# Edge passes of a graph kernel: three eight-slot loop bodies and one four-slot body with their own buffers, in place of one eight-slot body

## The chip, the cores and the metric

One Trainium2 chip, one of its cores. The metric is device time in microseconds (us) of one execution; lower is better. Time before: 10095.14 us, the median of 3 runs (10087.63 to 10098.26).

## What is computed

Four graph layers run one after the other on 3125 nodes of width 128 and 103125 directed edges (`src`, `dst`, sorted by `dst`), in fp32. All need, for each node, a weighted sum over the rows of the nodes that point at it:

```python
# layer 0: relation-aware attention; keys get the embedding of the edge's type (64 types)
# layer 1: three rounds of GAT convolution, 8 heads of 16
e = leaky_relu(e_src[src] + e_dst[dst], 0.2)
w = exp(e - segment_max(e, dst)[dst])
out = segment_sum(h[src] * (w / segment_sum(w, dst)[dst]), dst) + b
# layer 2: attention whose scores take features of the edge (64 attributes, a distance)
# layer 3: a sum of neighbours, scaled by 1/sqrt(degree) on both sides
```

Ahead of each layer stands a normalisation, behind it a residual sum.

## The kernel before

The nodes are sorted by degree and cut into NB = 25 blocks of 128, one node per partition. The edges of a block stand in *slots*: slot s of partition p is the s-th incoming edge of node p. A block has as many slots as its busiest node has edges, rounded up to 8. The chunk of work is SLOTS = 8 slots, that is 8 x 128 edges, in two halves of HALF = 4. Chunk boundaries by block stand in `bounds` (made at lines 499 to 526), at least 2 chunks per block and 3 in the last. The index lists are in DRAM: `el_idx`, `el_msk`, `el_typ`, one entry per chunk (written at lines 884 to 997).

`edge_pass` (from line 1542) is called six times: pass 0 (layer 0), passes 1 to 3 (the convolutions), pass 4 (layer 2) and pass 5 (layer 3). A pass reads a table of node rows in DRAM and writes the next table. Each engine runs a loop of its own over blocks and chunks, tied to the others by semaphores:

- **SP** (SyncE) loads the indices of a half, line 1582, `idx` h, when the gathers of the chunk before have landed; in pass 0 also the types (1587), in pass 4 `first` (1591) and the mask (1595).
- **POOL** (GpSimd) waits for the indices (1554) and for the half's landing buffer to be free (1556), then issues 4 indirect gathers (1558), each one row per partition; in pass 4 one gather of features per chunk (1565). Behind the gathers of block b it issues the scatter of block b-1's new rows (1444).
- **ACT** (ScalarE) copies the landed half into `work` (1384, 1391, 1402), which needs `work_free`, frees the landing buffer, and does the exponential (1285). In its chunk loop `step` (1671) the order is: one-hot of the types of chunk j+1 (`act_onehot`, 1368 and 1374, pass 0 only), exponential of chunk j, copy of chunk j+1. In passes 1 and 2 it also turns a tile of edge features per block (804 to 840), inside the first step of the next block.
- **PE** (TensorE) in pass 0 makes the keys of a half in `make_k` (1728): four matmuls of one-hot and type embeddings (1738) and one that adds the gathered keys (1743); it does so one chunk ahead of VectorE. At a block's end it does the projections (1071, 1074).
- **DVE** (VectorE) does the scores (1299, 1303 in passes 0 and 4; 1324, 1326 in 1 to 3), the running maximum (1273), the shift (1275), the weighing (1289) and the sum over slots (1294), after which the chunk's result is in slot 8 of `work`. At a block's end follow normalisation, projection and the new table rows (1151 to 1260).

There is one set of landing buffers (`land0`, `land1`, `land2`, two halves each), of `idx` (two halves), `first`, `msk` and `feat`. So the gathers of a half of chunk j+1 wait until ACT (or, in pass 5, DVE at 1358) has taken the same half of chunk j.

ACT's chunk step before:

```python
def step(j):
    if types: act_onehot(act)
    act_weights(act)
    act_copy(act, j + 1, landed)
```

## Time and profile before

| What | Value |
|---|---|
| median of the runs | 10095.14 us |
| the profiled execution | span 10072.8 us |
| POOL busy | 5899.5 us (59%) |
| DVE busy | 4386.1 us (44%) |
| PE, ACT busy | 1840.1 us (18%), 1435.6 us (14%) |
| granted TensorE clock | 1.00 throughout |
| DMA | 560.52 MB, mean 56 GB/s |
| first gather of passes 0 to 5 at | 920.5, 2572.4, 4049.4, 5507.1, 7015.9, 8706.1 us |
| last instruction | 10067.8 us |
| gathers, line 1558 | 5568, which is 6 passes x 116 chunks x 8 |

The span is one profiled execution from the first to the last instruction; the runs are timed on their own and their median is 22 us above it. Busy time counts instructions on an engine, not the waits between them, so no share here is a bound by itself; the passes are 91% of the span.

### The profile page before, as it was taken

How to read it: one execution, taken by the hardware profiler on the slowest of the kernel's cores; microseconds unless marked ns; L12 is line 12 of the kernel's file. 1: busy time of each engine (PE TensorE's matmuls, PEld its weight loads, DVE VectorE, ACT ScalarE, POOL GpSimd, SP SyncE). 2: the span in 40 equal slices, each digit the busy share in tenths (PEclk: the TensorE clock that was granted, in tenths of full speed). 3: DMA queues.
4: the chain of work that ended last, by engine and by line, in shares of the span. 5: the costliest groups of instructions: out<-in, count | busy, mean ns of one | idle time of the engine just before them, and what ended most of it. 6: DMA issues, size and time to landing. Idle time of an engine off the chain costs nothing. (4 is left out here: it accounts for less than half of the span.)

```text
span 10072.8 us, 74038 instructions
## 1 busy us (share of the span) xinstructions
PE 1840.1 (18%) x8000; PEld 1190.9 (12%) x8001; DVE 4386.1 (44%) x9101; ACT 1435.6 (14%) x3285; POOL 5899.5 (59%) x5959
## 2 busy tenths in 40 slices
PE   4334666666111111011111000000000000000000
PEld 4232333333000111000011000000000000000000
DVE  9314555555444444344444444444344444322222
ACT  0210222222111111111111111111111111000000
POOL 0113656555566666666666666665666665566666
DMA  0232434434333323323323322222312222222222
GB/s 17 38 48 52 99 96 99 97 93 97 51 58 57 57 57 61 53 57 58 57 60 57 48 47 48 49 47 41 43 43 43 42 46 40 39 47 46 48 45 44
DMA packets 612542, 560.52 MB, mean 56 GB/s; under 512 B 465184, under 2 KB 477759, under 8 KB 612390
## 3 DMA queue, kind: packets, MB, share of 16 engines
q0 software_dynamic: 205232, 477.48, 25.1%
q1 hardware_dynamic: 372836, 42.79, 3.2%
q10 hardware_dynamic: 34449, 40.02, 1.4%
q14 instruction: 21, 0.16, 0.0%
q8 instruction: 4, 0.07, 0.0%
HBM read 535.16 MB, written 24.61 MB: 56 GB/s over the span
## 5 line engine op out<-in xcount | busy, mean ns | idle before, releaser
L1558 POOL DMA_INDIRECT land<-table,idx x5568 | 5535.7, 994 | 3181.0 <-issue 1681.7
L1294 DVE TENSOR_REDUCE work<-prod 128x136 f32<-128x1224 f32 x464 | 1089.6, 2348 | 67.8 <-DVE prod L1289 0.2
L1071 PE MATMUL bank<-ident,hid 128*128 128x128 f32 x175 | 78.1, 446 | 4874.0 <-issue 2764.6
L1289 DVE TENSOR_TENSOR prod<-work,wt 128x1224 f32<-128x1224 f32 x464 | 665.5, 1434 | 639.5 <-DVEq L1279 410.6
L1391 ACT ACTIVATE work<-land 128x576 f32<-128x576 f32 x696 | 475.1, 683 | 2311.7 <-DMA land<-table,idx 2029.9
L1358 DVE TENSOR_REDUCE land<-land 128x128 f32<-128x640 f32 x232 | 285.7, 1231 | 1018.9 <-DMA land<-table,idx 830.9
L1324 DVE TENSOR_TENSOR sc<-work,own 128x64 f32<-128x64 f32 x348 | 81.2, 233 | 1327.2 <-issue 550.3
L1071 PEld LDWEIGHTS bank<-ident,hid 128*128 128x128 f32 x175 | 31.8, 182 | 5032.1 <-issue 5032.1
L1738 PE MATMUL bank<-rel,onehot 64*128 64x128 f32 x1856 | 511.7, 452 | 358.6 <-PEq L1736 278.0
L1738 PEld LDWEIGHTS bank<-rel,onehot 64*128 64x128 f32 x1856 | 449.9, 324 | 655.4 <-issue 655.4
L1743 PE MATMUL bank<-land,ident 128*128 128x512 f32 x464 | 481.0, 1140 | 108.3 <-DMA land<-table,idx 103.6
L1284 ACT ACTIVATE sc<-top 128x8 f32<-128x8 f32 x580 | 120.9, 208 | 2435.0 <-ACTq L1283 1651.9
L1299 DVE TENSOR_TENSOR kk<-work,own 128x512 f32<-128x512 f32 x232 | 160.8, 693 | 542.9 <-DVEq L1334 271.7
L1303 DVE TENSOR_REDUCE sc<-kk 128x32 f32<-128x512 f32 x464 | 318.3, 686 | 42.4 <-DVE kk L1299 0.8
L1299 DVE TENSOR_TENSOR kk<-bank,own 128x512 f32<-128x512 f32 x232 | 160.5, 692 | 379.2 <-DVEq L1314 194.5
L1444 POOL DMA_INDIRECT table<-stage,stage_i x150 | 149.2, 994 | 272.5 <-POOLq L1443 235.9
L1402 ACT ACTIVATE work<-land 128x512 f32<-128x512 f32 x232 | 145.5, 627 | 697.8 <-DMA land<-table,idx 647.8
L1384 ACT ACTIVATE work<-land 128x544 f32<-128x544 f32 x232 | 149.7, 655 | 591.7 <-DMA land<-table,idx 366.4
L363 POOL DMA_INDIRECT info_d<-inf,rank_i x25 | 24.2, 970 | 347.4 <-POOLq L361 340.1
L820 PE MATMUL bank<-b_ft,ones 1*125 1x176 f32 x150 | 69.4, 563 | 816.7 <-PEq L818 668.2
L870 POOL DMA_INDIRECT rec<-rec_id,at_i x25 | 23.7, 949 | 309.9 <-POOLq L869 309.9
L1273 DVE TENSOR_REDUCE top<-sc 128x8 f32<-128x72 f32 x580 | 162.3, 280 | 32.9
(285 smaller groups left out, 3855.0 us busy)
## 6 DMA issues: line engine op xcount, KB each, us to landing
land<-table,idx POOLq DMA_INDIRECT x5568
typ<-el_typ SPq DMA_DIRECT2D x232, 128.0 KB
attr<-in_edge_attr ACTq DMA_DIRECT2D x75, 343.8 KB
idx<-el_idx SPq DMA_DIRECT2D x1392, 2.0 KB
rec_ft<-fts ACTq DMA_DIRECT2D x75, 85.9 KB
near<-dist_t ACTq DMA_DIRECT2D x75, 62.5 KB
table<-stage,stage_i POOLq DMA_INDIRECT x150
first<-el_idx SPq DMA_DIRECT2D x116, 1.0 KB
```

Of the source, the lines that this page charges most:

```text
L1273: dve.tensor_reduce(top[:], sc[:].rearrange("p s h -> p h s"), AX.X, ALU.max).then_inc(ch.semaphore, ch.one())
L1289: dve.tensor_tensor(prod[:].rearrange("p s (h v) -> p s h v", h=HEADS), work[:, :, 0:HV].rearrange("p s (h v) -> p s h v", h=HEADS), wt[:] ...
L1294: dve.tensor_reduce(work[:, SLOTS, 0:HV], prod[:].rearrange("p s c -> p c s"), AX.X, ALU.add).then_inc(ch.semaphore, ch.one())
L1299: dve.tensor_tensor(kk[h][:], keys, slots(queries, HALF), ALU.mult).then_inc(ch.semaphore, ch.one())
L1303: dve.tensor_reduce(sc[:, h * HALF:(h + 1) * HALF, :], kk[h][:].rearrange("p s (h d) -> p s h d", h=HEADS), AX.X, ALU.add).then_inc(ch.sem ...
L1358: dve.tensor_reduce(land2[1 - h][:, HALF, :], land2[h][:].rearrange("p s c -> p c s"), AX.X, ALU.add).then_inc(ch.semaphore, ch.one())
L1384: act.activation(work[:, h * HALF:(h + 1) * HALF, 0:HV], land0[h][:, :, D:W0], ACT.Copy).then_inc(s(f"rows_free{h}"), 1)
L1391: act.activation(work[:, h * HALF:(h + 1) * HALF, :], land1[h][:], ACT.Copy).then_inc(s("act_chain"), 1)
L1444: pool.indirect_dma_start(target, bass.IndirectOffsetOnAxis(ap=stage_i[0:rows].bitcast(U32), axis=0), stage[0:rows], None).then_inc(s("tab ...
L1558: pool.indirect_dma_start(rows[h][:, k, :], None, source, bass.IndirectOffsetOnAxis(ap=idx[h][:, k:k + 1].bitcast(U32), axis=0)).then_inc( ...
L1738: last = pe.matmul(ps_rel[h][:, k * D:(k + 1) * D], onehot[mine, :, k], rel[mine], start=k == 0, stop=False, skip_group_check=True)
L1743: pe.matmul(ps_rel[h][:].rearrange("p (s d) -> p s d", d=D), ident[:], rows[h][:, :, 0:D], start=False, stop=True, skip_group_check=True). ...
```

## The change

The passes are walked with four loop bodies instead of one. Each has its own `idx`, `first`, `msk`, `feat` and landing buffers and its own semaphores:

- bodies a, b and c take 8 slots, body d takes 4 (the second half's place in `work`, `sc` and `prod`, so its DVE and ACT instructions cover 4 slots plus the running one);
- a block's slots are rounded up to 4, at least 28. With q = slots/4 - 7, the pair a, b runs (q>>2)+1 times, c ((q>>1)&1)+1 times, d (q&1)+1 times. Every block therefore takes a, b, c, d, and some repeat c, d or the pair. The counts are made on the device once (`quads`, `turns_at`) and read from SBUF by each engine at every block.
- ACT's order per body is one-hot, copy, exponential, with nothing for the body after it; the feature work of passes 1 and 2, and `act_after` in pass 3, stand behind the last body of a block. PE makes the keys of a block inside that block and no longer ahead; its feature work stands ahead of the block's projection.
- SP reloads `idx` of a body when ACT (DVE in pass 5) tells that it has seen the gathers landed, where it used to wait for the landing itself; PE too is told by ACT (`keys_in`).
- Pass 5 reduces each half into `part` and adds it to `acc`, where it used to take the running sum as a fifth slot.
- Setup gets some twelve small DVE instructions and four matmuls more, and one instruction more per run of 64 slots.

```diff
+        BODIES = {"a": (0, 1), "b": (0, 1), "c": (0, 1), "d": (1,)}
+        PLACES = [(x, q) for x, qs in BODIES.items() for q in qs]
+        idx = {(x, q): sb(f"idx_{x}{q}", [P, HALF], I32) for x, q in PLACES}
...
+        land = {(x, q): sb(f"land_{x}{q}", [P, HALF * W0]) for x, q in PLACES}
...
+        def turns_of(engine, b):
+
+            q = engine.value_load(quads[0:1, bass.ds(b, 1)], min_val=FEWEST, max_val=2 * JMAX) - FEWEST
+            return ((q >> LOOP_SHIFT) + 1, ((q >> (LOOP_SHIFT - 1)) & 1) + 1) + (((q & 1) + 1,) if TAIL_HALF else ())
+
+        def walk(engine, b, body):
+
+            loops = zip([("a", "b"), ("c",), ("d",)], turns_of(engine, b))
+            for bodies, turns in loops:
+                with engine.Fori(0, turns):
+                    for x in bodies:
+                        body(x)
+
+        def walk_numbered(engine, b, body):
+
+            at = [engine.value_load(turns_at[0:1, n, bass.ds(b, 1)], min_val=0, max_val=JMAX) for n in range(3 if TAIL_HALF else 2)]
...
+        def act_landed(act, x, h, t):
+
+            act.wait_ge(landed(x, h), t * (16 * HALF) + 16 * HALF)
+            act.sem_inc(s(f"idx_free_{x}{h}"), 1)
...
+        def act_copy_l0(act, x, t):
+            for h in BODIES[x]:
+                act_landed(act, x, h, t)
+                act.sem_inc(s(f"keys_in_{x}{h}"), 1)
             act.wait_ge(s("work_free"), 1)
             act.sem_inc(s("work_free"), -1)
...
+                    with sp.Fori(0, NB) as b:
+                        j0 = sp.value_load(bounds[0:1, bass.ds(b, 1)], min_val=0, max_val=JMAX - 2 * RC)
+                        t = turns_of(sp, b)
+                        with sp.Fori(0, t[0]) as i:
+                            loads("a", j0 + i * 2)
+                            loads("b", j0 + i * 2 + 1)
+                        with sp.Fori(0, t[1]) as i:
+                            loads("c", j0 + t[0] * 2 + i)
+                        if TAIL_HALF:
+                            with sp.Fori(0, t[2]) as i:
+                                loads("d", j0 + t[0] * 2 + t[1], i)
...
-                        def step(j):
+                        def body(x, t):
                             if types:
-                                act_onehot(act)
-                            act_weights(act)
-                            act_copy(act, j + 1, landed)
...
+                                act_onehot(act, x)
+                            act_copy(act, x, t)
+                            act_weights(act, x)
+
+                        def block_end(b, more):
+
+                            if makes_features:
+                                act_copy_turned(act, 0)
+                                if more:
+                                    act_attr_load(act, 0, makes_features + b + 1)
+                                act_store_features(act, 0, makes_features + b)
+                            if act_after:
+                                act_after(act)
...
+                        with act.Fori(0, NB - 1) as b:
+                            walk_numbered(act, b, body)
+                            block_end(b, True)
...
+                        with pe.Fori(0, NB) as b:
                             if types:
+                                walk(pe, b, make_k)
                                 pe_project(pe, wo0[:], D)
+                            if makes_features:
+                                pe_turn_edges(pe, 0)
+                                pe_features(pe, 0)
+                            pe_after(pe)
```

## Rows read from the trace of the kernel before

**Rows 1.** The page's costliest groups: line engine op, tensors, count | busy us, mean ns | idle before

```profile
L1558 POOL DMA_INDIRECT land<-table,idx x5568 | 5535.7, 994 | 3181.0 <-issue 1681.7
```

**Rows 2.** The waits of POOL, one row per pass, passes 0 to 5: total us, times, longest

```profile
POOL land L1558 <- POOLq L1556: 376.5, 91, 7.1
...
POOL land L1558 <- POOLq L1556: 202.4, 38, 10.3
...
POOL land L1558 <- POOLq L1556: 173.4, 40, 9.1
...
POOL land L1558 <- POOLq L1556: 247.8, 32, 11.0
...
POOL land L1558 <- POOLq L1556: 256.9, 65, 12.7
...
POOL land L1558 <- POOLq L1556: 119.0, 29, 7.1
```

**Rows 3.** The tile sh in pass 0: duration min/median/max ns, first and last start

```profile
L1275 DVE TENSOR_TENSOR sh<-sc,top x116: 232/232/234, 936.8 to 2549.8; 128x72 f32<-128x72 f32 x116
```

**Rows 4.** Timeline of pass 0, one body: start us, us, engine line op, count [idle before]

```profile
1352.53 2.20 PE L1738 MATMUL bank<-rel,onehot 64*128 64x128 f32 x8 [3.47 <-PEq L1736]
...
1357.33 2.20 PE L1738 MATMUL bank<-rel,onehot 64*128 64x128 f32 x8 [0.60 <-PEq L1736]
...
1358.92 0.71 ACT L1368 ACTIVATE typ_d<-typ,neg_p 128x512 f32<-128x512 f32 x1
...
1359.47 2.07 PE L1743 MATMUL bank<-land,ident 128*128 128x512 f32 x2
1359.89 0.63 ACT L1374 ACTIVATE onehot<-typ_d 128x512 f32<-128x512 f32 x1 [0.27 <-ACTq L1373]
...
1362.47 0.69 DVE L1299 TENSOR_TENSOR kk<-bank,own 128x512 f32<-128x512 f32 x1 [0.18 <-DVEq L1314]
...
1364.34 0.23 DVE L1275 TENSOR_TENSOR sh<-sc,top 128x72 f32<-128x72 f32 x1
...
1364.87 0.25 ACT L1285 ACTIVATE wt<-sh 128x72 f32<-128x72 f32 x1
```

**Rows 5.** Timeline of pass 1, end of a block and start of the next

```profile
3990.47 0.25 ACT L1285 ACTIVATE wt<-sh 128x72 f32<-128x72 f32 x1
...
4001.51 0.32 ACT L837 ACTIVATE fts<-bank 125x176 f32<-125x176 f32 x1 [0.55 <-issue]
4002.10 0.31 ACTq L840 DMA_DIRECT2D rec_ft<-fts  x1
...
4008.43 0.25 ACT L1285 ACTIVATE wt<-sh 128x72 f32<-128x72 f32 x1
...
4013.53 0.23 DVE L1324 TENSOR_TENSOR sc<-work,own 128x64 f32<-128x64 f32 x1 [0.66 <-DVEq L1323]
...
4014.36 0.23 DVE L1275 TENSOR_TENSOR sh<-sc,top 128x72 f32<-128x72 f32 x1
```

**Rows 6.** Timeline of pass 2, from the fourth gather of a half to its copy

```profile
4053.18 0.95 POOL L1558 DMA_INDIRECT land<-table,idx  x1 [0.31 <-issue]
...
4055.77 0.68 ACT L1391 ACTIVATE work<-land 128x576 f32<-128x576 f32 x1 [8.32 <-DMA land<-table,idx]
```

**Rows 7.** Timeline of pass 5, an index load and the gather behind it

```profile
9517.01 3.51 SPq L1582 DMA_DIRECT2D idx<-el_idx  x2
...
9520.31 0.96 POOL L1558 DMA_INDIRECT land<-table,idx  x1 [5.00 <-issue]
```

**Rows 8.** Timeline of pass 0, end of a block on VectorE and TensorE

```profile
1339.57 0.17 DVE L1151 TENSOR_SCALAR den<-work 128x8 f32<-128x8 f32 x1 [0.80 <-DVEq L1640]
...
1348.24 0.82 PE L1074 MATMUL bank<-w_g,hid_t 128*128 128x144 f32 x2 [0.63 <-PEq L1073]
```

**Rows 9.** Timeline of pass 4, VectorE, last shift of a block and first of the next

```profile
7219.38 0.23 DVE L1275 TENSOR_TENSOR sh<-sc,top 128x72 f32<-128x72 f32 x1
...
7241.19 0.23 DVE L1275 TENSOR_TENSOR sh<-sc,top 128x72 f32<-128x72 f32 x1
```

More of the change, by code:

```diff
@@ L39 @@
 KEYSTEP = 4096
+TAIL_HALF = True
+UNIT = HALF
+FEWEST = 7
+LEAST = 4
+LOOP_SHIFT = 2
 class Chain:
@@ L171, in program @@
         bounds = sb("bounds", [1, NB + 1], I32)
-        counts = sb("counts", [1, NB], I32)
+        quads = sb("quads", [1, NB], I32)
+        turns_at = sb("turns_at", [1, 3, NB + 1], I32)
         rbounds = sb("rbounds", [1, NB + 1], I32)
@@ L1015, in program, with rows_of, first_slot, landed @@
         prod = sb("prod", [P, SLOTS + 1, HV])
-        land0 = [sb(f"land0{h}", [P, HALF, W0]) for h in range(2)]
-        land1 = [sb(f"land1{h}", [P, HALF, W1]) for h in range(2)]
-        land2 = [sb(f"land2{h}", [P, HALF + 1, D]) for h in range(2)]
+        land = {(x, q): sb(f"land_{x}{q}", [P, HALF * W0]) for x, q in PLACES}
+        acc = sb("acc", [P, D])
+        part = sb("part", [P, D])
+        def rows_of(x, q, width):
+            return land[x, q][:, 0:HALF * width].rearrange("p (s c) -> p s c", c=width)
+        def first_slot(x):
+            return HALF * BODIES[x][0]
+        this_pass = [0]
+        def landed(x, h):
+            return s(f"rows_in{this_pass[0]}_{x}{h}")
+        def turns_of(engine, b):
[9 more added lines that the diff above has]
+            at = [engine.value_load(turns_at[0:1, n, bass.ds(b, 1)], min_val=0, max_val=JMAX) for n in range(3 if TAIL_HALF else 2)]
+            loops = zip([("a", "b"), ("c",), ("d",)], turns_of(engine, b), at)
+            for bodies, turns, t in loops:
+                with engine.Fori(0, turns) as i:
+                    for x in bodies:
+                        body(x, t + i)
         def dve_rsqrt(dve, ch, v, to, t, one_column=True):
@@ L1304, in dve_scores_sum, with chunk_l0 @@
             dve.wait_ge(ch.semaphore, ch.count)
-        def dve_mask(dve, ch):
-            dve.tensor_tensor(now, now, msk[:].unsqueeze(2).broadcast_to([P, SLOTS, HEADS]), ALU.add).then_inc(ch.semaphore, ch.one())
-            dve.wait_ge(ch.semaphore, ch.count)
-            dve.sem_inc(s("msk_free"), 1)
-        def chunk_l0(dve, ch, b, j, landed):
-            for h in range(2):
+        def chunk_l0(dve, ch, b, x, t):
+            for h in BODIES[x]:
                 dve.wait_ge(s(f"rel_ready{h}"), 1)
@@ L1327, in chunk_conv, with chunk_l2 @@
             dve.wait_ge(ch.semaphore, ch.count)
-            dve_weights(dve, ch)
-            dve_weigh(dve, ch)
-        def chunk_l2(dve, ch, b, j, landed):
-            for h in range(2):
+            dve_weights(dve, ch, x)
+            dve_weigh(dve, ch, x)
+        def chunk_l2(dve, ch, b, x, t):
+            f = first_slot(x)
+            n = SLOTS - f
+            now = sc[:, f:SLOTS, :]
+            for h in BODIES[x]:
                 dve.wait_ge(s("copied"), 1)
@@ new lines, in _ @@
+                    for x, h in PLACES:
+                        sp.wait_ge(s(f"idx_free_{x}{h}"), 1)
+                        sp.sem_inc(s(f"idx_free_{x}{h}"), -1)
+                    for x in BODIES:
+                        if mask:
+                            sp.wait_ge(s(f"msk_free_{x}"), 1)
+                            sp.sem_inc(s(f"msk_free_{x}"), -1)
+                        if features:
+                            sp.wait_ge(s(f"first_free_{x}"), 1)
+                            sp.sem_inc(s(f"first_free_{x}"), -1)
```

452 lines of the change are left out of this document (216 added, 236 removed).

## The prediction

> **What bounds it now.** I start with the page's costliest groups: the gathers on POOL are the largest by far, 5568 at 994 ns [rows 1], and each is followed by 0.30 us of issue, so one takes 1.25 us when nothing holds it back and a chunk of eight 10.0 us. The other engines are busy for less than half of a pass. Then the waits of POOL, pass by pass [rows 2]: 376.5, 202.4, 173.4, 247.8, 256.9 and 119.0 us at line 1556, which is the wait for a landing buffer. Waits for indices are small beside these. So a pass is its gathers, plus 1376 us in all in which POOL stands still because the one set of buffers has not been emptied. In pass 0 the body is long for another reason as well, and there I read the shifts, one per chunk: 116 from 936.8 to 2549.8 us [rows 3], 1613 us for 115 steps, 14.0 us each. The granted clock is 1.00 throughout, the level of 2.4 GHz, and plays no part.
>
> **How many gathers.** The counts come from the inputs: sorted by degree, the 25 blocks' largest degrees give 116 chunks of 8 (the trace has 5568/48 = 116) and, rounded up to 4 and at least 28, 884 slots where there were 928. As bodies that is 58 of a and b, 35 of c, 35 of d: 128 bodies, 93 of eight slots and 35 of four. 44 gathers fewer per pass save 44 x 1.25 = 55 us. Pass 4 has 12 feature gathers more, +15. Ten blocks run c twice and ten run d twice (four of these both); three run the pair a, b more than once.
>
> **Pass 0: the new order on ACT puts the one-hot on the chain.** Before, ACT makes the one-hot of chunk j+1 before the exponential of chunk j, so PE makes the next keys while VectorE weighs. In the change the one-hot of a body stands behind the exponential of the body before, and nothing of the next body can start earlier on PE. The step from exponential to exponential is then a plain sum [rows 4]: from the end of the exponential, about 0.1 and then Square and Relu with the gap between them, 1358.92 to 1360.52, 1.6; about 0.4 to PE; keys of both halves, 1352.53 to 1361.54, 9.0 (4.8 per half, 1352.53 to 1357.33, the last without the gap); from there to the second half's scores 0.9 (1361.54 to 1362.47); to the start of the shift 1.9; to the end of the exponential 0.8 (1364.34 to 1365.12). That is 14.6 us; for body d, one half less, 9.8. Copies, typ loads and gathers (10.6 us for eight) fit beside it. At a block's end: sum over slots of a short body 3.3, the block's end 1339.57 to 1349.06, 9.5, of which some 3 go since PE no longer makes a half of the next keys in it [rows 8]; PE's turn of its loop, 1.5 as an estimate; then 12.5 of the sum above from PE's start on: 23.8. So pass 0 takes 68 x 14.6 + 35 x 9.8 + 24 x 23.8 = 1907 us where it took 1613 [rows 3]: **+294 us**, with bounds +230 and +340 for the estimates in it. No faster buffer helps here, and the 376.5 us of POOL's waits [rows 2] only become longer ones.
>
> **Passes 1 to 3: what is left of POOL's waits.** Let A be the time from the last exponential of a block to the first of the next. Before, one such stretch took 18.0 us (3990.47 to 4008.43), and a body in between, exponential to exponential, can go in 6.5 (4008.43 to the shift at 4014.36, and 0.5) [rows 5], well below POOL's 10.0. The four bodies let POOL run ahead over 28 slots, 35 us, so a stretch A is hidden unless a body is repeated. A repeated body has to wait: its indices are reloaded only when ACT has seen the last ones landed. Landing takes 1.6 us from the end of the fourth gather (4054.13 to 4055.77) [rows 6], an index load with the start of the gather 3.3 (9517.01 to 9520.31) [rows 7], so a d behind a d costs at least 1.6 + 3.3 - 0.3 = 4.6 us of POOL. With POOL's start on a block as zero, the last exponential is near 4, the first of the block at 4 + A, ACT copies the first c once b is weighed, near A + 12, and POOL, done with c at 31 with its scatter, can repeat it at A + 15: A - 16 is lost; in the same way A - 15 where d repeats. How long is A? The 18.0 held some 10 in which ACT waited for the next chunk to land before it did the block's features; that wait goes. Then come its feature work (8, an estimate, no row of mine), the block's register work, which was 6.0 for two reads (4002.41 to 4008.43) [rows 5] and now has four reads, 8 to 16, I take 10; and copy, scores and exponential, 6: A = 24. Its bounds are 19, where the reads cost next to nothing, and 31, where they and the rest run at the slow pitch. With 24: ten times 8, ten times 9, and some 20 where a short block of 28 slots is bound by A + 17 instead of 37: 190 us of waits per pass. So -55 - 202 + 190 = **-67**, -55 - 173 + 190 = **-38**, and -55 - 248 + 190 = **-113**; pass 3 gains most as its logarithm no longer waits for the next chunk.
>
> **Pass 4.** A was 21.8 (7219.38 to 7241.19) [rows 9]; with a read more and ACT idle at the block's end I take 24. The body takes 7.1 on VectorE beside 11.3 on POOL, the mask and `first` have buffers of their own, and repeats cost 2 to 4 each: 100 us of waits with the short blocks. -55 + 15 - 257 + 100 = **-197**. **Pass 5.** VectorE's work is short; what is left are the ten repeats of d at 4.6 or more, as SP's index loads come late there at times [rows 7], and little for c: 85. -55 - 119 + 85 = **-89**. **Setup** gets the small instructions and one more for each of 25 runs: +8, between 0 and +20. Splitting the sum of pass 5 in two is hidden behind the gathers, with 5 us per half to do 1.6.
>
> **The sum.** +294 - 67 - 38 - 113 - 197 - 89 + 8 = -202. The profiled execution's 10072.8 would become 9871; the median lies 22 above it and I carry that over: 10095 - 202 = 9893 us.
>
> **A rule that speaks against it.** Runs of instructions fetched anew: in the trace a body's jump back costs 0.66 us of VectorE's time, 4012.87 to 4013.53, and the start of a block 6.0 on ACT [rows 5]; which of it is fetching, no row tells. The Trainium skill (Runtime: NRT & Kernel Launch, section Instruction fetch mechanics) says that prefetch is sequential and that a taken branch to a target outside the two pages held makes the sequencer load that page first. Loops four times as long are more likely to leave those pages; by that rule the jump to the next block would stall on each engine. What that would make is the third rival.
>
> **The rivals.** (1) *The block's start is short, A = 19.* Repeats then cost 3 to 5, waits fall to some 75 per pass, pass 4 to 60, pass 5 to 60: 345 + 40 + 25 = 410 more saved, 9480. For it: POOL's own start of a block costs nothing visible. Against it: 6.0 us for two reads. (2) *The block's start is long, A = 31.* Each us above 24 costs 20 to 25 us in each of passes 1 to 4, for ten c, ten d and the short blocks, so 7 us cost 560 to 700, of which pass 4, bound less by ACT, takes a third: some 480 in all, 10370. It decides from A = 26.2, where 90 per us have eaten the 202. The place is ACT's chain at each block: reads of `turns_at`, features, first copy. For it: ACT now does all of this with nothing to overlap. (3) *Code is loaded again at each block.* 100 blocks of passes 1 to 4, each with a load as long as an index load, 2.5 to 3.3 [rows 7], on ACT or VectorE: A grows by 3, +270: 10160. (4) *Pass 0 is not held by the one-hot*, for a reason that I don't see: then it falls to its gathers, 1105 us and some 130: 9893 - 670 = 9220.
>
> **Chances.** Forecast 0.48, with a range of its own of 9700 to 10060; (1) 0.20; (2) 0.18; (3) 0.09; (4) 0.05. The range for 8 in 10 leaves out (4), the far half of (2) and a little of (1): 9450 to 10320. Under 0.2% is 20 us, about what can be told from no change here. Faster by more than that: nearly all of the forecast's own range and (1) and (4): 0.69. Same: 0.05. Slower: 0.26, from (2), (3) and the forecast's upper end.
>
> **What the profile after would show.** Gathers: 5304. Pass 0 longer, near 1910 from first to last shift, exponentials 14.6 apart inside a block, PE idle between a body's keys and the next; if they are 12 or less apart, my main step is wrong. Waits of POOL in passes 1 to 3 near 190 each and only at repeated c and d; if they stand at every block, A is above 31. From the last exponential of a block to the first of the next 24 us, ACT busy with registers for some 10 of it. Pass 4 near 1490, pass 5 near 1275.

## The result and the profile after

The changed kernel takes 11020.6 us (median of 4, 11015.18 to 11029.99) where the kernel before takes 10091.4 beside it: ratio 1.0921 [1.0906, 1.0937]. The forecast was 9893. The page of the profiled execution answers to [rows 1] like this; the columns are the same:

```profile
span 11019.3 us, 83988 instructions
...
PE 1776.2 (16%) x7898; PEld 1167.7 (11%) x7899; DVE 4353.2 (40%) x9661; ACT 1432.7 (13%) x3386; POOL 5575.8 (51%) x5707
...
L1710 POOL DMA_INDIRECT land_c<-table,idx_c x1680 | 1642.0, 977 | 1640.8 <-POOLq L1708 1120.4
L1710 POOL DMA_INDIRECT land_a<-table,idx_a x1392 | 1390.4, 999 | 752.1 <-issue 383.0
L1710 POOL DMA_INDIRECT land_b<-table,idx_b x1392 | 1347.0, 968 | 479.6 <-issue 405.9
L1710 POOL DMA_INDIRECT land_d<-table,idx_d x840 | 808.3, 962 | 1382.9 <-POOLq L1708 1140.4
```

There are 5304 gathers, as forecast, each about as long as before (0.98 us on average, 0.99 before), and no engine is busier. The idle time of POOL has grown from 3181 to 4256 us, and most of it stands before c and d, at line 1708, the wait for a landing buffer. The stretches of the six passes, each from its first gather (start and end, length, busy time and instructions of PE, PEld, DVE, ACT and POOL, granted clock, share of DMA, GB/s):

```profile
919.00:2925.00 2006.00, 993.36 (x2366) 573.94 (x2366) 933.64 (x1605) 351.66 (x734) 896.98 (x909) 1.00 0.31 75
2925.00:4613.30 1688.30, 181.69 (x675) 148.94 (x675) 613.85 (x1093) 247.62 (x628) 902.82 (x910) 1.00 0.24 48
4613.30:6286.10 1672.80, 180.42 (x670) 147.89 (x669) 612.72 (x1093) 247.45 (x628) 901.75 (x910) 1.00 0.24 48
6286.10:7888.30 1602.20, 51.60 (x75) 17.06 (x75) 706.53 (x1467) 277.05 (x603) 896.77 (x909) 1.00 0.22 42
7888.30:9657.80 1769.50, 30.30 (x75) 17.06 (x75) 738.56 (x2415) 219.58 (x605) 1012.53 (x1038) 1.00 0.20 38
9657.80:11019.30 1361.50, 0.00 (x0) 0.00 (x0) 312.47 (x541) 0.00 (x0) 863.01 (x909) 1.00 0.21 44
```

Against the kernel before that is +354, +211, +215, +93, +79 and -5 us, where I had +294, -67, -38, -113, -197 and -89.

**Where it went: the start of a block.** I read the time from the last exponential of a block to the first of the next, A in the prediction, 24 times in each of passes 0 to 4. Means in us:

```
                pass 0   1     2     3     4
kernel before    21.3  19.6  18.6  22.2  23.9
changed          26.4  35.5  34.8  28.8  33.0   (forecast 23.8, then 24)
```

One such stretch on ACT, pass 3, behind a block that repeated d (start us, us, line, operation, idle time before it):

```profile
7261.32 0.22 ACT L1358 ACTIVATE wt<-sh 128x40 f32<-128x40 f32 x1
7266.79 0.31 ACT L1279 ACTIVATE tmp<-tmp 128x128 f32<-128x128 f32 x1 [5.25 <-issue]
...
7268.81 1.28 ACT L1283 ACT_TABLE_LOAD   x1
7284.39 0.68 ACT L1478 ACTIVATE work<-land_a 128x576 f32<-128x576 f32 x1 [14.30 <-issue]
7289.31 0.68 ACT L1478 ACTIVATE work<-land_a 128x576 f32<-128x576 f32 x1 [4.23 <-issue]
7294.90 0.21 ACT L1357 ACTIVATE sc<-top 128x8 f32<-128x8 f32 x1 [4.91 <-issue]
```

14.3 us before the first copy, and "issue" says that ACT waited for nothing the profile knows. What it did are the four reads of the block's numbers, two moves and the look at a semaphore ahead of the copy. The same stretch for lines 1089 and 1076 (operation and count: duration ns min/median/max, first and last start):

```profile
L1089 ACTq SEQ_ASSERT  x3: 18/124/1392, 7268.2 to 7273.8; - x3
...
L1076 ACTq TENSOR_LOAD <-quads x1: 699/699/699, 7276.6 to 7276.6; - x1
L1076 ACTq FUSED_REGOPS  x1: 690/690/690, 7278.0 to 7278.0; - x1
L1076 ACTq SEQ_ASSERT  x1: 708/708/708, 7279.4 to 7279.4; - x1
```

Instructions that elsewhere take 0.28, 0.15 and 0.02 us take 0.7 each here from 7269.6 us on, and most start 1.4 us apart; the first few, up to then, are quick. Behind a block in which nothing was repeated the same instructions are quick, and the stretch is 17.3 us:

```profile
7673.84 0.22 ACT L1358 ACTIVATE wt<-sh 128x40 f32<-128x40 f32 x1
...
7681.38 1.28 ACT L1283 ACT_TABLE_LOAD   x1
7682.99 0.69 ACT L1478 ACTIVATE work<-land_a 128x576 f32<-128x576 f32 x1 [0.33 <-issue]
...
7691.01 0.21 ACT L1357 ACTIVATE sc<-top 128x8 f32<-128x8 f32 x1 [5.86 <-issue]
```

By blocks, pass 3: 16 stretches behind a block with a repeated c or d last 28 to 40 us (mean 33), the five behind a block a, b, c, d 17 to 19, and the three behind a repeated pair a, b 20, 25 and 30. The split is not as clean elsewhere: in pass 1 of the same trace the five take 28 to 30 us (with a repeat 32 to 42), and in e12 below, the same program, those of pass 3 take 17 to 24 and one behind a repeated c and d takes 17. Sequencer instructions of 0.65 to 0.73 us, counted over the trace on ACT, DVE and SP: 660, 353 and 1368 in the kernel before, 1561, 523 and 1458 in the changed one.

In passes 1 and 2 two more things lie in the stretch. DVE waits for its transposed row (first two rows), and ACT issues its loads, waits for PE's features and then reads (last two). Of the 24.8 us ahead of line 877 the first 8.4 are ACT's own loads, at the slow pitch, and 16.1 are the wait for PE:

```profile
3948.82 0.29 DVE L1249 TENSOR_TENSOR hid<-tmp,b_g 128x128 f32<-128x128 f32 x1
3973.21 0.29 DVE L1157 COPY hid_t<-bank 128x128 f32<-128x128 f32 x1 [24.09 <-DVEq L1156]
```

```profile
3971.19 0.32 ACT L877 ACTIVATE fts<-bank 125x176 f32<-125x176 f32 x1 [24.76 <-ACTq L874]
...
3983.13 0.68 ACT L1478 ACTIVATE work<-land_a 128x576 f32<-128x576 f32 x1 [11.63 <-ACTq L1475]
```

POOL's waits for the buffers of c and d in pass 1 (total us, times, longest); 384 of these 399 us stand at a repeated c or d, which is what a long A must give:

```profile
POOL land_c L1710 <- POOLq L1708: 206.3, 13, 23.1
POOL land_d L1710 <- POOLq L1708: 193.0, 16, 28.2
```

### The profile page after: what moved, and what is told of

Same layout as the page of the kernel before. It is cut to its first block and busy times, and to the rows that moved or that the text cites. A ratio compares the mean times of both kernels' runs of the same rounds, so it can differ in the third digit from the quotient of the medians.

```text
span 11019.3 us, 83988 instructions
## 1 busy us (share of the span) xinstructions
PE 1776.2 (16%) x7898; PEld 1167.7 (11%) x7899; DVE 4353.2 (40%) x9661; ACT 1432.7 (13%) x3386; POOL 5575.8 (51%) x5707
## 5 line engine op out<-in xcount | busy, mean ns | idle before, releaser
L1710 POOL DMA_INDIRECT land_c<-table,idx_c x1680 | 1642.0, 977 | 1640.8 <-POOLq L1708 1120.4
L1710 POOL DMA_INDIRECT land_a<-table,idx_a x1392 | 1390.4, 999 | 752.1 <-issue 383.0
L1710 POOL DMA_INDIRECT land_b<-table,idx_b x1392 | 1347.0, 968 | 479.6 <-issue 405.9
L1710 POOL DMA_INDIRECT land_d<-table,idx_d x840 | 808.3, 962 | 1382.9 <-POOLq L1708 1140.4
L1368 DVE TENSOR_REDUCE work<-prod 128x136 f32<-128x1224 f32 (+1 forms) x512 | 1064.8, 2080 | 74.8
L1363 DVE TENSOR_TENSOR prod<-work,wt 128x1224 f32<-128x1224 f32 (+1 forms) x512 | 655.7, 1281 | 365.6 <-DVEq L1351 200.7
L1396 DVE TENSOR_TENSOR sc<-work,own 128x64 f32<-128x64 f32 (+1 forms) x384 | 84.1, 219 | 1195.1 <-DVEq L1395 536.6
L1157 DVE COPY hid_t<-bank 128x128 f32<-128x128 f32 x175 | 51.1, 292 | 1033.1 <-DVEq L1156 510.4
L1533 POOL DMA_INDIRECT table<-stage,stage_i x150 | 161.4, 1076 | 459.0 <-POOLq L1532 427.3
L1478 ACT ACTIVATE work<-land_a 128x576 f32<-128x576 f32 x174 | 118.8, 683 | 915.5 <-ACTq L1475 400.7
L1478 ACT ACTIVATE work<-land_c 128x576 f32<-128x576 f32 x210 | 143.6, 684 | 521.9 <-DMA land_c<-table,idx_c 310.6
```

The lines of the kernel that those rows point to most:

```text
L1363: dve.tensor_tensor(prod[:, f:].rearrange("p s (h v) -> p s h v", h=HEADS), work[:, f:, 0:HV].rearrange("p s (h v) -> p s h v", h=HEADS), ...
L1368: dve.tensor_reduce(work[:, SLOTS, 0:HV], prod[:, f:].rearrange("p s c -> p c s"), AX.X, ALU.add).then_inc(ch.semaphore, ch.one())
L1396: dve.tensor_tensor(now, work[:, f:SLOTS, HV:W1], slots(blk(own1, b, W1, W1 + HEADS), n), ALU.add).then_inc(ch.semaphore, ch.one())
L1478: act.activation(work[:, h * HALF:(h + 1) * HALF, :], rows_of(x, h, W1), ACT.Copy).then_inc(s("act_chain"), 1)
L1533: pool.indirect_dma_start(target, bass.IndirectOffsetOnAxis(ap=stage_i[0:rows].bitcast(U32), axis=0), stage[0:rows], None).then_inc(s("tab ...
L1710: pool.indirect_dma_start(rows_of(x, h, width)[:, k, :], None, source, bass.IndirectOffsetOnAxis(ap=idx[x, h][:, k:k + 1].bitcast(U32), ax ...
```

## The experiments

They were run on five chips. The kernel before, timed on each beside the variants, took 9351 (e1 to e4), 9317 (e5 to e8), 10077 (e9 to e11), 10054 (e12 to e15) and 9407 us (e16 to e18): two kinds, and I call the 10050 to 10090 kind, on which the result above was measured, the first. Ratios are to the kernel before on the same chip. Each chip was seen in one session only, so "chip" may also mean the moment.

**The changed kernel on another chip, and again on one of the first kind.** No edit.

> The changed kernel, unchanged, beside the kernel before and the variants. In the runs of e1 to e4 the kernel before took 9351 us where it had taken 10091, and their traces show next to none of the 0.7 us instructions on SP, ACT and DVE. Theory 1 (these slow instructions belong to the chip or the moment, not to a variant's edit): where the kernel before takes 9350, the changed one takes 9270 to 9300, its distance across a block 23, 15, 15, 17 and 20 us in passes 0 to 4; where the kernel before takes 10090, it takes 11020 again, with distances 26, 35, 35, 29 and 33. Theory 2 (the variants' edits removed them): 11020 whatever the kernel before takes.

> The kernel before, for a trace from the same chip as the others. Theory 1 (slow instructions come with the chip or the moment, and cost the kernel before less than the changed one): where it takes 9350, its distances across a block are the fully quick ones, 4 to 7 us under those of the first trace in passes 1 to 4 (21.3, 19.6, 18.6, 22.2, 23.9), slow instructions near none. Theory 2 (it is something else, gathers or clock): its pitch of gathers inside a half or the granted clock differs from 1.25 us and 1.00.

> The changed kernel unchanged, as the measure of this chip. Theory 1 (there are two kinds of chips for this kernel): it is at 1.09 of the kernel before where that takes about 10080, and at 0.995 where it takes about 9330, and nothing between. Theory 2 (it was the moment, not the chip): a ratio between these two, or another one at the same time of the kernel before.

e5: 9270.2 us, 0.9952 [0.9935, 0.9969]. e12: 10982.0, 1.0935 [1.0913, 1.0958]. So the same program is 9% slower on one kind and 0.5% faster on the other. The passes of e5:

```profile
908.30:2815.30 1907.00, 993.42 (x2366) 573.88 (x2366) 933.48 (x1605) 351.38 (x734) 880.53 (x909) 1.00 0.31 79
2815.30:4094.10 1278.80, 181.80 (x675) 148.94 (x675) 613.26 (x1093) 246.88 (x628) 924.25 (x909) 1.00 0.30 63
...
5374.10:6656.50 1282.40, 51.62 (x75) 17.08 (x75) 706.73 (x1467) 276.75 (x603) 923.89 (x909) 1.00 0.25 53
6656.50:8071.00 1414.50, 30.34 (x75) 17.09 (x75) 737.65 (x2415) 219.36 (x605) 1034.07 (x1037) 1.00 0.22 48
```

The busy times of PE, DVE and ACT are those of the first chip within 1 us in passes 0 to 4, the clock too; only the lengths differ. The kernel before in e6, whose passes are 1562.6, 1319.8, 1341.4, 1452.8, 1518.2 and 1228.0 us, is shorter as well; its distances fall by the 4 to 7 us expected in passes 1, 2 and 4, but by only 1.9 in pass 3. Against it the changed one makes +344, -41, -61, -170, -104 and -30. The reads of line 1089 over the whole of e5, and a stretch of ACT in pass 3 after the same block as the first one above:

```profile
L1089 ACTq FUSED_REGOPS  x615: 46/152/178, 904.6 to 8003.1; - x154
L1089 ACTq TENSOR_LOAD <-turns_at x375: 272/279/1029, 904.1 to 8002.8; - x188
L1089 ACTq SEQ_ASSERT  x375: 18/18/33, 904.8 to 8003.2; - x188
```

```profile
6160.22 1.28 ACT L1283 ACT_TABLE_LOAD   x1
6161.86 0.68 ACT L1478 ACTIVATE work<-land_a 128x576 f32<-128x576 f32 x1 [0.36 <-ACTq L1475]
```

The 14.3 us are 0.36 us. Distances across a block, means:

```
                     pass 0   1     2     3     4
e6, kernel before     21.3  12.8  12.8  20.3  19.3
e5, changed           22.8  15.3  15.4  17.2  19.4
e12, changed (first)  26.2  35.6  35.1  29.2  32.5
```

Slow instructions on ACT, DVE and SP: 73, 1, 1 in e6, 88, 26, 0 in e5. From the second kind to the first the changed kernel's span grows by 1751 us, and its distances across a block by 24 x (3.6 + 20.2 + 19.4 + 11.6 + 13.6) = 1640; of the 743 us of the kernel before, by 24 x (0 + 6.8 + 5.8 + 1.9 + 4.6) = 460. The two don't match pass by pass: passes 1 and 2 grow by 410 and 393 us where their distances grow by 485 and 466, and pass 5, in which ACT does nothing, grows by 164.

**c and d once.** The repeat bits are masked, here and in `turns_at`, so the edges of the repeats are left out.

```diff
-            return ((q >> LOOP_SHIFT) + 1, ((q >> (LOOP_SHIFT - 1)) & 1) + 1) + (((q & 1) + 1,) if TAIL_HALF else ())
+            return ((q >> LOOP_SHIFT) + 1, ((q >> (LOOP_SHIFT - 1)) & 0) + 1) + (((q & 0) + 1,) if TAIL_HALF else ())
```

> Edit: c and d run once in every block (their repeat bits are masked), so the edges of the repeats are left out: 10 bodies c and 10 bodies d per pass. What the left-out bodies alone take off, by their distances in the changed kernel's trace: pass 0 10 x 14.6 + 10 x 12.0, passes 1 to 3 10 x 13.1 + 10 x 9.4 each, pass 4 10 x 13.5 + 10 x 10.8, pass 5 120 gathers at 1.25: 1330 us in all. Theory 1 (after a block whose c or d was repeated, the instructions of ACT at the block's end and the next one's start come 0.7 to 1.4 us apart; without a repeat they do not): the distance across a block falls from 33 to about 17 in pass 3, from 36 to about 22 in pass 4, from 38 to 28 in passes 1 and 2, from 30 to 23 in pass 0, for 16 of 24 blocks: another 870 us, total near 8820. Theory 2 (the start of a block is long whatever ran before, by the number of register reads and the work on ACT and DVE): distances across a block stay where they are, total near 9690.

> c and d once in every block, edges of the repeats left out, as in e1, where it took 7991 us beside 9351 and, with 1330 us of bodies left out, had nothing else to gain. Where the kernel before takes about 10080: theory 1 (the repeated loop ahead of a block's end makes the instructions behind it slow): distances across a block fall to 17 in pass 3, 19 to 25 in pass 4, 23 in pass 0 and 26 to 30 in passes 1 and 2, total 8600 to 9000. Theory 2 (the slow instructions come with the block's end, repeated or not): distances stay at 26, 35, 35, 29 and 33, total near 9690. Where it takes about 9330: 7990 again.

e1: 7991.0 us, 0.8543. That is 1279 less than e5 (another chip of its kind), near the 1330 of the left-out bodies, and its distances across a block are 22.6, 15.0, 15.2, 17.1 and 19.2, as in e5: next to no slow instructions there (84 on ACT), nothing more to gain. e13, on the first kind: 8930.2, 0.8888 [0.8873, 0.8903], 2052 below e12, so some 720 more than the bodies. Distances: 22.6, 28.3, 29.2, 23.0 and 23.3 against e12's 26.2, 35.6, 35.1, 29.2 and 32.5. The total is within the 8600 to 9000 of theory 1. A repeated c or d adds to the stretch behind it, but isn't all: in pass 3, 16 of the 24 stretches take 24 us where I expected 17, with 7 to 11 slow instructions on ACT in each, and the count of slow instructions on ACT over the whole is still 977 (1457 in e12).

**a, b walked last.**

```diff
-            for bodies, turns in loops:
+            for bodies, turns in (c, d, a):
```

> Edit: every engine walks c, then d, then the pair a, b, so in 22 of 25 blocks no loop is repeated just ahead of the block's end. Where the kernel before takes about 10080: theory 1 (what was repeated last decides): distances across a block fall towards those of blocks without a repeat (17 in pass 3, 23 in pass 0), about 10 us in 16 of 24 blocks of five passes, given back in part where a repeated c waits for its gathers right behind the block's start (6 us in 10 blocks), total 10300 to 10600. Theory 2: no change, 10900 to 11100. Where it takes about 9330: distances across a block stay, a repeated c comes behind fewer gathers made ahead, 0 to 150 us more than 9270.

10734.3 us, 1.0679 [1.0658, 1.0699], 248 less than e12 beside it. Distances: 24.2, 24.7, 24.1, 21.8 and 26.0. They fall by about 11 us in passes 1 and 2 and by 7 in 3 and 4, which is theory 1's direction, though 22 to 26 us are left. The total lies between the two theories' ranges: the distances give some 900 us, and all but 248 are lost again, since others grew: a to b in passes 1 to 4 to 9.5 to 11.2 us where it was 6.9 to 7.8, and from the last d to a 9 to 16 us, where the loop's end before a new body took 7 to 9 (14 in pass 0).

**Where the loops stand.** So in all passes for the block loops of ACT, DVE, SP and PE:

```diff
-                        with act.Fori(0, NB - 1) as b:
+                        with nc.Fori(0, NB - 1, engines=[act.engine], head_slot={act.engine: 0}) as b:
```

> Edit: the block loops of ACT, DVE, SP and PE in all six passes are placed so that their first instruction stands at slot 0 of a 256-instruction fetch block; nothing else changes. Theory 1 (the slow instructions come from where the loops happen to lie in the program, so that each trip needs code from another block): slow instructions go, passes 3 and 4 lose about 15 us at 16 blocks each, total near 10300 or below. Theory 2 (they come with the branches themselves, wherever the code lies): distances stay within 2 us, total 10950 to 11100.

> Block loops of ACT, DVE, SP and PE placed at slot 0 of a 256-instruction fetch block, as in e4. Where the kernel before takes about 10080: theory 1 (the place of the loops makes their instructions slow): total near 10300 or below, slow instructions of ACT under 400 of the 1561. Theory 2 (the branches make them slow wherever the code lies): within 100 us of the changed kernel, slow instructions of ACT as many as there. Where it takes about 9330: the changed kernel's time, as in e4.

e4: 9288.1, 0.9933 [0.9916, 0.9949]. e15: 11034.4, 1.0968 [1.0945, 1.0990], with 1493 slow instructions on ACT beside 1457 in e12. The place of the block loops' heads is not the cause; the heads of the loops inside a block weren't placed.

**More instructions at the head of ACT's block.**

```diff
+                        with act.Fori(0, NB - 1) as b:
+                            with act.Fori(0, 20):
+                                act.value_load(quads[0:1, bass.ds(b, 1)], min_val=0, max_val=2 * JMAX)
```

> Edit to the changed kernel: at the head of each of 24 blocks in passes 0 to 4, ACT reads one value 20 times in a small loop, about 12 us of its time (0.45 us for load, copy and check, 0.15 us for the loop's own), as slow instructions would take. On this kind of chip the changed kernel takes 0.995 of the kernel before. Theory 1 (at the block's head ACT is on the chain that starts the next block, since its copy, its exponential and the features all come behind it): distances across a block grow by 8 to 12 us in passes 1 to 4 and 3 to 7 in pass 0, a third of it is given back where POOL has gathered ahead, total 9900 to 10200. Theory 2 (DVE's chain at a block's end or the gathers hide it): under 3 us per block, total under 9500.

> The same 20 reads at the head of each block on ACT of the kernel before, where they stand behind the copy of the block's first chunk. Theory 1 (the kernel before bears a delay on ACT better than the changed one, since its copy is done ahead of it): distances across a block grow by 5 to 8 us in passes 1 to 4 and by under 2 us in pass 0, total 9317 + 350 to 650. Theory 2 (both bear it alike, and the changed kernel lost on the first chip only because it has more such instructions): the growth of the total is within 15 per cent of that of the changed kernel.

> Edit: ACT reads the three values of turns_at once more at the head of each block (12 more instructions in 24 blocks of passes 0 to 4), and uses them for nothing. Theory 1 (instructions there cost 0.7 to 1.4 us each on the chain, where a body was repeated before): 16 blocks x 5 passes x 12 x about 1.2 us = 1150 us less what passes 1 and 2 hide, total 11600 to 12200. Theory 2 (a read costs what it costs in a quick stretch, 0.5 us for load, copy, check and copy): 24 x 5 x 1.6 = 190 us, total 11210. Theory 3 (the reads lie beside DVE's chain and are hidden): 11020.

> Twelve more instructions on ACT at the head of each block, as in e3. Where the kernel before takes about 10080: theory 1 (each comes 0.7 to 1.4 us after the one ahead, on the chain): distances across a block grow by 8 to 17 us in blocks with a repeated c or d and hardly in the others, total 12000 to 12600 less what passes 1 and 2 give back, at least 1.15 of the kernel before. Theory 2 (slow instructions are a fixed stretch of time after the branch, not a price per instruction): growth under 3 us per block, total under 11350. Where it takes about 9330: 0.993 to 0.998 again.

e9 and e10 came to the first kind of chip, so their totals aren't those expected for the other. There 20 reads took ACT about 24 us in e9 and 18 in e10 (medians, first to last). e9: 12985.0, 1.2888 [1.2863, 1.2913], against 1.0921 without them: some 1980 us more, 16.5 per block. e10: 11643.0, 1.1553 [1.1534, 1.1572], 1565 more, 13 per block, and there too distances across a block grow, by 8 in pass 0 and 17 in pass 1. So instructions at this place are on the chain in both kernels, and per us of them one bears it no better than the other (about 0.7 of ACT's time for them reaches the total in both). That is theory 2 of e10 in its mechanism, but by its own mark, growths within 15%, it missed: they are 21% apart.

The trace of e9 also says how the slow pitch ends. Turn by turn of the small loop, the time from read to read is, as means of 120 blocks, 3.2, 3.3, 2.8, 2.2, 2.0, 1.9 and 1.4 us for the first seven turns, 0.8 to 0.9 for all later ones, and turns 11 to 14 are quick in every block; in e10 it is 2.7, 1.6 and 1.0, then 0.8 to 1.0. The same instructions are thus slow in the first turns and quick later, so the slow pitch at a block's start is a stretch that passes, not a price of each instruction. 20 reads at 0.82 us are 16.4 us, and 16.5 per block is what e9 costs. Twelve more instructions on the second kind do nothing that the totals can tell, e3 0.9929 [0.9912, 0.9946], e16 0.9892 [0.9876, 0.9909]: the distances grow by 1.6 us in passes 1 and 2 and by none elsewhere (e3); e16's ratio is just under the 0.993 to 0.998 expected. Twelve on the first kind weren't timed, since e16 came to the second, but e9's turns there speak for e16's theory 2.

**PE's order and ACT's wait for the features.** e2 moves the projection (first hunk); e7 puts it between `pe_turn_edges` and `pe_features`, and has ACT store a block's features behind the next block (second hunk):

```diff
+                            pe_after(pe)
                             if makes_features:
                                 pe_turn_edges(pe, 0)
                                 pe_features(pe, 0)
-                            pe_after(pe)
...
+                                if not first:
+                                    act_store_features(act, 0, makes_features + b - 1)
                                 act_copy_turned(act, 0)
...
+                                else:
+                                    act_store_features(act, 0, makes_features + b)
```

> Edit: on PE, the block's projection stands ahead of the feature work again. The changed kernel's DVE waits 13 to 24 us for its transposed row in passes 1 and 2. Theory 1 (DVE's wait for the projection is what makes a block's start long there): the distance across a block falls by about 15 us in 48 blocks, total near 10300. Theory 2 (ACT waits for the same features before it goes on to the next block's copy, so it ends no earlier): DVE's wait goes, the distance across a block stays within 2 us of 37, total 10950 to 11050.

> Edit: in passes 1 and 2, ACT stores the features of a block behind the next block, so it no longer waits for PE's feature matmuls at a block's end, and PE does the projection ahead of these matmuls. Theory 1 (where instructions are slow, this wait of 8 us on ACT and the projection's 13 to 24 us behind PE's features make the start of a block long in passes 1 and 2): distance across a block from 35 to about 24, 48 x 11 = 530 us off, total near 10500 on a slow chip. Theory 2 (ACT's own slow instructions, ten for the loads of attributes and sixteen register reads, fill 30 us anyway): 3 to 5 us per block, 150 to 250 us off, near 10820. On a quick chip either gives under 60 us off the 9290.

e2: 9442.4, 1.0099 [1.0082, 1.0116], worse than the changed kernel: distances in passes 1 and 2 go from 15.3 to 22.5. The turned attributes, for which ACT waited nowhere in e5, now come behind the projection on PE, and ACT waits 7.0 us a block for them; the row of pass 1 of e2, where e5 has 0.0:

```profile
L849 ACT ACTIVATE a_t<-bank 128x500 f32<-128x500 f32 x25 | 14.7, 587 | 175.6 <-ACTq L848 175.6
```

So a new wait takes the place of the removed one (DVE's for its row fell from 72.7 to 20.7 us), and costs more. Neither run came to the first kind, for which e2's totals and the larger gains of e7 were forecast. e7: 9237.1, 0.9915 [0.9899, 0.9932], 33 us below e5 beside it, distances 12.7 and 12.9, within the 60 us that it gave for this kind. Its edit is also in e11, on the first kind. ACT's idle time ahead of the store in the changed kernel's pass 1 on the first chip (busy us, mean ns, idle before it):

```profile
L877 ACT ACTIVATE fts<-bank 125x176 f32<-125x176 f32 x25 | 7.9, 318 | 484.9 <-ACTq L874 318.5 <-ACTq L876 148.3 <-issue 18.1
```

and in e11:

```profile
L877 ACT ACTIVATE fts<-bank 125x176 f32<-125x176 f32 x25 | 8.0, 318 | 38.1 <-issue 27.1 <-ACTq L876 8.4
```

The 19 us per block, of which 8 were ACT's own loads and 11 the wait for PE, are gone from this place, and the distances are 33.2 and 34.8 where they were 35.5 and 34.8. ACT's slow instructions fill the time: in passes 1 and 2 there are 18 and 19 of them in a stretch where there were 10 and 9, and it waits for semaphores for 3 us of it where it was 14. An expected gain that a second late step takes back.

**The one-hot's order in pass 0.**

```diff
-                            if types:
+                            if types and x != "b":
                                 act_onehot(act, x)
                             act_copy(act, x, t)
+                            if types and x == "a":
+                                act_onehot(act, "b")
```

> Edit: in pass 0 ACT makes the one-hot of body b ahead of the exponential of body a, as the kernel before did for every body. Theory 1 (the one-hot behind the exponential is what sets 14 us between two exponentials of pass 0): 29 distances from a to b fall from 14.0 to 10 or 11 us, about 100 us off. Theory 2 (PE's keys and DVE's scores set the distance whatever the order): 14.0 stays, total within 15 us of the changed kernel's.

9150.2, 0.9821 [0.9804, 0.9837], 120 us below e5: the 29 distances from a to b went from 13.98 to 9.82, all others stayed, and 29 x 4.16 = 121. So the one-hot behind the exponential is what makes pass 0 long.

**Both orders back, and then a, b last as well.** All bodies load both halves of types, and one load of types more closes the pass; the store of e7 is in it, and in e18 the order of e14.

```diff
-                            if types:
-                                act_onehot(act, x)
                             act_copy(act, x, t)
+                            if types:
+                                act_onehot(act)
                             act_weights(act, x)
```

> The changed kernel with two orders of the kernel before put back: in pass 0, the one-hot of the body that comes next is made ahead of the exponential in every body (all bodies load both halves of types, one load more at the end), and in passes 1 and 2 the features of a block are stored behind the next block (as in e7). Theory 1 (the order of ACT in pass 0 sets 14.2 us between exponentials, here 9.8 as from a to b in e8): another 39 distances of 14.2 fall to 9.8, 35 of 9.5 and 12 to about 7 and 9, those across a block from 22.8 to 21.3; with the 33 us of e7 that is 0.95 of the kernel before, near 8870 where that takes 9317. Theory 2 (with the order back, gathers or the wait for a repeated c set the pass): pass 0 ends no lower than the kernel before's 1523 us from first to last exponential, total near 8980.

> Both orders of the kernel before put back, as in e11, where the kernel before took 10077 and this one 1.065 of it. There again 1.06 to 1.07. Where the kernel before takes about 9330: pass 0's distances of 14.2 fall to about 10, total 0.95 to 0.965 of the kernel before.

> e17 with c, d, then a, b walked, as in e14. Where the kernel before takes about 10080: e14 took 250 us off the changed kernel and e11 another 290; both together near 10450, 1.04 of the kernel before, so no version here beats it on that kind. Where it takes about 9330: e17's time or up to 100 us above it, since a repeated c comes behind fewer gathers made ahead.

e11, first kind: 10730.5, 1.0652 [1.0619, 1.0685]; its pass 0 is 1771 us, against 2006 in the changed kernel and 1652 in the kernel before. e17: 8937.6, 0.9500 [0.9484, 0.9516]; pass 0 is 1581 us from gather to gather, its exponentials about 10.3 apart, the best version of all on the second kind. e18: 9179.5, 0.9761, 242 us more than e17 where I allowed 100. A repeated c right behind the block's start waits for its gathers, 13.0 and 13.5 us in passes 1 and 2 instead of 10.5, but that is some 55 us; the largest loss, 81 us, is in pass 3, where a to b went from 6.7 to 10.1 us and the distance across a block from 17.2 to 18.6. Nothing that I ran beats the kernel before on the first kind.

## Why the prediction was wrong

- **Gathers** (5304, 1.25 us apart): right.
- **Pass 0**: right in mechanism, e8 shows it. Inside a block I had 14.6 and 9.8, and 14.2 to 14.6 and, to a first d, 9.5 were measured. The shifts answer to [rows 3]:

```profile
L1347 DVE TENSOR_TENSOR sh<-sc,top x128: 199/232/268, 936.9 to 2897.7; 128x72 f32<-128x72 f32 x93, 128x40 f32<-128x40 f32 x35
```

  1961 us where I had 1907. The distance across a block, 26.4 instead of 23.8, made 61 us and the ten repeated d, at 12.0 instead of 9.8, another 22; the other bodies took 29 less. On the second kind the distance is 22.8.
- **A, the start of a block, is the step that failed.** I took 24 with bounds 19 and 31. Measured: 35, 35, 29 and 33 in passes 1 to 4 of the chip of the result, and 15, 15, 17 and 19 on the other kind; no pass of either is within 4 us of 24. The sum for A had three terms, and each can be read (means of 24 stretches, us: from a block's last exponential to ACT's first read, which is the features in passes 1 and 2 and the logarithm in pass 3; from there to the first copy, the reads; from the copy to the exponential):

```
                      features   reads   copy to exponential
the sum for A              8      10      6
changed, pass 1         24.6     7.4    3.5
         pass 2         24.4     7.0    3.4
         pass 3          7.7    13.4    7.7
         pass 4          3.9     9.7   19.4
e5,      pass 1          8.6     3.2    3.5
         pass 3          6.4     2.8    8.1
         pass 4          0.6     2.8   16.0
```

  In passes 1 and 2 the mis-sized term is the feature work, "8, an estimate, no row of mine": 24.5 us, of which some 8 are ACT's own loads, slow, and 12 the wait for PE's features. On the second kind it is 8.6, so the estimate was right for a chip without slow instructions. The reads took 7 us there on average, less than the 10 priced, and were too cheap only in pass 3, at 13.4, within the bound of 16 (up to 24 in single blocks). Pass 4's 24 had no such terms; there the copy to the exponential is 19.4. The one stretch of the kernel before from which I priced two reads at 6.0 us [rows 5] already held instructions at both pitches, so its 6.0 was no price of quick reads.
- **The waits at repeated c and d** (A - 16 and A - 15) hold in passes 1 and 2 when the measured A is put in: 10 x 19 + 10 x 20 = 390 us in each, where 384 and 385 were measured at the repeats; in pass 3 they give 266 and 310 were measured. On the second kind, with A at 15, only the 4.6 us at a repeated d should be left, 46 us, and 44 stand there; the row of pass 1 of e5 is

```profile
POOL land_d L1710 <- POOLq L1708: 51.1, 24, 4.8
```

- **Passes 4 and 5, setup**: pass 4 has the same failed A (33). Pass 5 gained 5 and 30 us on the two kinds, not 89. It has no ACT, but DVE reads the four values there. On the first kind POOL still waits 155.9 us for d's buffers, 62 us of idle time at a repeated d and 102 at the first d of a block, which I had at nothing and whose cause stays open. On the second kind 44 us are left at the ten repeats, 4.4 each, but there the kernel before had only 35 us of such waits to lose. Setup +8 came out as -2 and +1, and the 22 us carried over from the span to the median were 1.
- **The rivals.** It was rival 2, at the place named, ACT's chain at a block's start, with the sign named, and larger: at its own 90 us for each us of A above 24, a mean A of 33 gives 9893 + 810 = 10700, and pass 0's 54 more 10760; of the 260 us left, pass 5 is 84. Its chance of 0.18 was too low, and the range cut off its far half. I had said that waits at every block would put A above 31; A is above 31 in passes 1, 2 and 4, but in passes 1 to 3 the waits stand at the repeats. On the second kind it was rival 1, a short start, at 15 to 19; but there the kernel before is quicker by 743 us as well, so the gain came to 0.5% and not to the 6% of that rival.
- **Rival 3**, code loaded anew at each block, by the rule of the Trainium skill (Runtime: NRT & Kernel Launch, section Instruction fetch mechanics). The profile of the changed kernel counts the packets of the instruction queues (packets, MB, share):

```profile
q14 instruction: 36, 0.29, 0.0%
q8 instruction: 3, 0.05, 0.0%
```

  The kernel before has 21 and 4. That is far from one per block and engine, and e5 has the same 36 and 3 on the kind of chip where next to nothing is slow. So loads of pages as the rule has them don't make the difference between the kinds. Nor do they fit e9, where the same few instructions of a small loop stay slow for up to seven turns. What makes the difference, these packets don't show.

Shown, then: where most of the 9% are (the distance across a block), what fills them (sequencer instructions 0.7 and 1.4 us apart, and in passes 1 and 2 a wait for PE whose removal alone gains next to nothing), that on the kind of chip without them the same program is 0.5% faster, and that leaving the repeats out (e13) or moving them (e14) shortens the stretch. Open: why one kind of chip has them and the other not, why more stand behind a repeated loop, and pass 5's waits at the first d.

## What to carry to other kernels

Count the sequencer instructions (reads, checks, branches, DMA issues) that stand alone on the chain between two blocks, and look in the trace for ones of 0.7 us before pricing them: buffers that hide 35 us of gathers are worth little if the engine that empties them spends 33 us on its way into the next block. Give each term of such a stretch a row of its own: the one that failed here was the one without a row. Work that was done ahead across a loop's end (the one-hot, the first copy, a store of the block before) has a price when the loop is restructured, here 4.2 us per body in pass 0. And a kernel whose blocks begin with register work should be timed on more than one chip, with the kernel before beside it each time.

## What the runs showed of the hardware that I had not expected

- Sequencer instructions on SP, ACT and DVE can take 0.69 to 0.71 us each instead of 0.02 to 0.28. They mostly start 1.4 us apart, whether another engine has slow ones beside or not: in the changed kernel, of pairs on ACT with none on DVE, SP or POOL beside, 534 are 1.4 apart and 137 are 0.7. Where ACT and DVE both have them, they can start together (7156.96 and 7158.36 us on both in pass 3).
- It comes with the chip or the session: 1561, 1457 and 1493 on ACT in the changed kernel, e12 and e15 on the first kind, 88 and 83 in e5 and e4 on the second.
- They stand behind repeated loops more than elsewhere: 28 to 40 us against 17 to 19 across a block in pass 3 of the changed kernel, 31 to 40, but for one block of 17, against 17 to 24 in e12.
- They pass: in e9 the turns of one small loop of reads fall from 3.2 to 0.82 us within seven turns.
- PE's rows are no witness of it, but what waits for PE is. In the stretch above PE's transpose is recorded from 3951.41 for 0.47 us, and the copy that waits for it starts at 3973.21. On average that copy starts 15.2 and 16.2 us behind the transpose's recorded end in passes 1 and 2 of the changed kernel, 0.1 in e5, 0.2 or less in the kernel before on the first kind and 0.1 in e11, where the transpose comes ahead of the feature matmuls. So PE is late there too, behind its feature matmuls; which of its instructions are, its rows don't show.
